# Four attention chunks in one program over a ring of adjacency blocks, in a graph network on one core

## The reference

```python
# layer 0: degree-normalized graph convolution
h = x @ W.T + b;  a = adj + I;  x = layernorm(x + (a * r[:, None] * r[None, :]) @ h)
# layer 1: attention; n = 3327 nodes, h = 8, and d = 128 is the batch of the einsum
q = (x @ Wq.T).reshape(d, n, h)      # k and v alike
a = einsum('dnh,dmh->dnm', q, k) * d ** -0.5 + adj + adj
out = einsum('dnm,dmh->dnh', softmax(a, axis=2), v).reshape(n, h * d) @ Wo.T
x = layernorm(x + out)
# layer 2: graph convolution with bias and relu;  layer 3: attention over edges, by exp and adj.T
```

## Time and profile before

| | us |
|---|---|
| median of three runs | 11376.24 (11374.95 to 11376.49) |
| the profiled execution, its own time | 11372.95 |
| its span | 11371.2 |
| TensorE / VectorE / ScalarE / GpSimd busy | 10347.5 / 9970.1 / 10362.4 / 8141.1 |
| first exponential of the attention to the start of its last one | 844.50 to 10817.38 |

### The profile page before, as it was taken

How to read it: one execution, slowest core, us unless ns; L and a number is a source line. 1 busy time by engine, 2 the same in 40 slices (tenths; PEclk the granted TensorE clock), 3 DMA queues, 4 the chain that set the end, 5 groups by cost and what they waited for, 6 DMA issues and landing times. The chain is left out here.

```text
span 11371.2 us, 371147 instructions
## 1 busy us (share of the span) xinstructions
PE 10347.5 (91%) x138582; PEld 5321.7 (47%) x138582; DVE 9970.1 (88%) x10702; ACT 10362.4 (91%) x8620; POOL 8141.1 (72%) x4114
## 2 busy tenths in 40 slices
PE   5749999999999999999799999999999999999988
PEld 4614555555545555555344444444444444444474
DVE  7348999999989999999799999999899999999958
ACT  3149999999999999999899999999999999999925
POOL 0007888888878888888688888888788888888800
PEclk7979999999999999999899999999999999999999
DMA  8694443433454433433433333333433333333364
GB/s 331 217 254 77 62 62 61 62 61 62 62 94 62 62 61 61 62 61 62 90 54 53 55 55 55 54 54 55 93 54 54 55 55 54 53 55 55 52 197 178
DMA packets 505827, 943.45 MB, mean 83 GB/s; under 512 B 100743, under 2 KB 453390, under 8 KB 454702
## 3 DMA queue, kind: packets, MB, share of 16 engines
q1 hardware_dynamic: 505740, 942.28, 42.4%
HBM read 799.88 MB, written 142.00 MB: 83 GB/s over the span
## 5 line engine op out<-in xcount | busy, mean ns | idle before, releaser
L1101 DVE SCALAR_TENSOR_TENSOR a_probs<-ps,a_adj 128x768 f32<-128x768 f32 (+1 forms) x9216 | 8976.8, 1020 | 776.3 <-PE ps L991 663.4
L1076 POOL TENSOR_TENSOR a_pool_probs<-a_pool_probs,a_adj 128x768 f32<-128x768 f32 (+1 forms) x4096 | 8124.6, 1984 | 1860.7 <-ACT a_pool_probs L1051 1860.7
L1056 ACT ACTIVATE a_probs<-a_probs 128x1536 f32<-128x1536 f32 (+3 forms) x4096 | 8207.4, 2004 | 12.6 <-DVE a_probs L1101 12.2
L991 PE MATMUL ps<-a_q,a_k 34*128 34x384 f32 (+1 forms) x26624 | 4457.4, 406 | 650.6 <-ACT a_pool_probs L1051 367.7
L1051 ACT ACTIVATE a_pool_probs<-ps 128x768 f32<-128x768 f32 (+1 forms) x4096 | 4486.9, 1095 | 32.6 <-PE ps L991 32.5
L1011 PE MATMUL ps<-a_probs,a_v 128*9 128x192 f32 (+1 forms) x73728 | 4012.9, 341 | 0.0
L991 PEld LDWEIGHTS ps<-a_q,a_k 34*128 34x128 f32 x26624 | 2180.5, 185 | 3179.4 <-ACT a_pool_probs L1051 1187.8
L1011 PEld LDWEIGHTS ps<-a_probs,a_v 128*9 128x9 f32 x73728 | 1952.1, 91 | 1273.0 <-issue 126.4
L1011 PE MATMUL ps<-a_pool_probs,a_v 128*9 128x192 f32 (+1 forms) x32768 | 2218.9, 343 | 2.3 <-POOL a_pool_probs L1076 2.2
L1011 PEld LDWEIGHTS ps<-a_pool_probs,a_v 128*9 128x9 f32 x32768 | 489.5, 89 | 986.3 <-issue 980.6
L571 POOL MEMSET v_rows<- 128x512 f32 x2 | 1.9, 1054 | 480.1 <-POOLq L83 480.1
(11 more groups left out here) (177 smaller groups left out, 2104.7 us busy)
## 6 DMA issues: line engine op xcount, KB each, us to landing
a_k<-k_parts SPq DMA_DIRECT2D x2048, 208.0 KB
a_v<-v_ext SPq DMA_DIRECT2D x512, 117.0 KB, 3.4
adj_t<-tr SPq DMA_DIRECT2D x26, 1664.0 KB, 6.4
g0tile<-adj_t SPq DMA_DIRECT2D x26, 1664.0 KB, 6.9
g2tile<-adj_t SPq DMA_DIRECT2D x26, 1664.0 KB, 7.0
nat<-in_adj SPq DMA_DIRECT2D x25, 1663.5 KB, 10.1
e_nat<-in_adj SPq DMA_DIRECT2D x25, 1663.5 KB, 6.8
a_q<-q_parts SPq DMA_DIRECT2D x2048, 12.0 KB
```

The costliest lines, as they stand in the source:

```text
L991: ins = nc.tensor.matmul(ps[:, place + bank:place + bank + half], k_tile[b][row:row + SCORE_ROWS, P * j:P * (j + 1)].bitcast(F32R), q_tile ...
L1056: nc.scalar.activation(sums, sums, ACT.Exp, scale=2.0).then_inc(sums_exped, 1)
L1076: nc.gpsimd.tensor_tensor(flat(k), flat(k), adj_c[:, j, :], ALU.mult).then_inc(multiplied, 1)
L1101: v.scalar_tensor_tensor(out=halves(flat(k)), in0=score(j), scalar=SCALE / 2, in1=halves(adj_c[:, j, :]), op0=ALU.mult, op1=ALU.add).then_ ...
```

## The change

One attention program runs all four chunks, in the same order. The adjacency lies in a ring of 32 blocks (`AdjRing`, `ADJ_SLOTS` = 26 + 6), each of one DMA: with six spare slots part 0 of a chunk (now six blocks) is loaded at the beginning of the chunk before it. Parts 0 and 1 of the first chunk are loaded in the bound phase, and the K tiles are set there too. The factors exp(2 adj) are made once, in the first graph layer, by ScalarE, from the tiles that are loaded there, and kept in the DRAM tensor `factors`; ring blocks of `POOL_BLOCKS` are loaded from it. At a switch K, Q and V of batch 1 are loaded between the parts. K and Q have a semaphore for each half, and stores one for each buffer. In the output phase wo and w2 are loaded behind the first and second row block, and VectorE divides row block 0 before it copies the transposed wo.

```diff
-CHUNK_GROUPS = ((0, 2, 7), (14, 2, 6))
+CHUNKS = ((14, 6), (20, 6), (0, 7), (7, 7))
+GROUPS_OF_CHUNKS = ((6, 2), (7, 2))
+WIDEST = 7
-ADJ_PARTS = ((0, 7), (7, 13), (13, 19), (19, BLOCKS))
+ADJ_PARTS = ((0, 6), (6, 13), (13, 19), (19, BLOCKS))
+ADJ_SLOTS = BLOCKS + 6
@@ gcn_phase, SP and ScalarE
-            with sp.Fori(0, BLOCKS // 2) as t:
-                for b in range(2):
+            for i in range(BLOCKS + 1):
+                b, t = i % 2, i // 2
+                if i < BLOCKS:
                     sp.wait_ge(acc_ready[b], t)
+                    if i >= 2:
+                        sp.wait_ge(made, 2 * (i - 1))
+                    sp.dma_start(tile[b][:, :, :].rearrange("p j q -> p (j q)"), flat_t[i]).then_inc(loaded[b], LOAD)
+                if i:
+                    sp.wait_ge(made, 2 * i)
+                    sp.dma_start(factors[i - 1], factor[1 - b][:, :, :]).then_inc(kept[1 - b], LOAD)
+            per = len(POOL_BLOCKS) // 2
+            for i in range(BLOCKS):
+                b, t = i % 2, i // 2
+                act.wait_ge(loaded[b], (t + 1) * LOAD)
+                if t:
+                    act.wait_ge(kept[b], t * LOAD)
+                for n in range(2):
+                    of = POOL_BLOCKS[per * n]
+                    nc.scalar.activation(factor[b][:, per * n:per * (n + 1), :], tile[b][:, of:of + 3 * per - 2:3, :],
+                                         ACT.Exp, scale=2.0).then_inc(made, 1)
@@ bound_phase, SP and GpSimd
+            for part in ring.EARLY:
+                ring.load(sp, 0, part, True)
+            for b in range(2):
+                nc.gpsimd.memset(k_tile[b][:, :], 1.0)
@@ AdjRing
+    EARLY = (0, 1)
+    def slot(self, c, j):
+        return (BLOCKS * c + j) % ADJ_SLOTS
+    def load(self, sp, c, part, factored):
+        first, nb = CHUNKS[c]
+        for j in range(*ADJ_PARTS[part]):
+            of = self.adj_t[first:first + nb, :, j, :]
+            if factored and j in POOL_BLOCKS:
+                of = self.factors[first:first + nb, :, POOL_BLOCKS.index(j), :]
+            sp.dma_start(self.block(c, j, nb * P).rearrange("p (i q) -> p i q", q=P), of.rearrange("i p q -> p i q")
+                         ).then_inc(self.loaded[part], LOAD)
@@ attention_phase, SP: beginning, and each chunk
-            sp.wait_ge(cleared, 3)
+            load(0, 0, 0)
             load_v(BATCHES - 1, 0)
+            for part in range(len(ADJ_PARTS)):
...
+                if not n_pool or part not in ring.EARLY:
+                    ring.load(sp, 0, part, n_pool > 0)
+            load(0, 1, 1)
             load_v(BATCHES - 2, 1)
+                if more:
+                    sp.wait_ge(ring.loaded[0], ring.ready(c, 0, n_pool > 0))
+                    if c:
+                        used(c - 1, BLOCKS)
+                    ring.load(sp, c + 1, 0, n_pool > 0)
...
                     all_scored(done - 1)
-                    load(0, 0, then)
+                    load(c + 1, 0, 0)
                     sp.wait_ge(batch_summed, done - 1)
                     load_v(BATCHES - 1, 0)
+                    used(c, ADJ_PARTS[1][1] - spare)
+                    ring.load(sp, c + 1, 1, n_pool > 0)
+                sp.wait_ge(stored[1], (done // 2 - 1) * per_store)
+                store(c, done, BATCHES - 2, 0)
                 if more:
+                    used(c, ADJ_PARTS[2][1] - spare)
+                    ring.load(sp, c + 1, 2, n_pool > 0)
                     all_scored(done)
+                    load(c + 1, 1, 1)
+                    used(c, ADJ_PARTS[3][1] - spare)
+                    ring.load(sp, c + 1, 3, n_pool > 0)
                     sp.wait_ge(batch_summed, done)
                     load_v(BATCHES - 2, 1)
@@ attention_phase, TensorE, ScalarE and GpSimd
-                    pe.wait_ge(loaded[b], (pair + of // 2 + 1) * per_load)
+                    for sem in loaded[b]:
+                        pe.wait_ge(sem, (pair + of // 2 + 1) * per_load)
-                        if factors and b == 0:
-                            act.wait_ge(adj_loaded[part_of[j]], (c + 1) * (nb * LOAD))
-                            nc.scalar.activation(adj_c[:, j, :], adj_c[:, j, :], ACT.Exp, scale=2.0
-                                                 ).then_inc(factored, 1)
-            for b in range(2):
-                nc.gpsimd.memset(k_tile[b][:, :], 1.0).then_inc(cleared, 1)
-                                if b == 0:
-                                    pool.wait_ge(factored, c * n_pool + (pool_rank[j] + 1))
+                                if b == 0 and j in (begin for begin, _ in ADJ_PARTS):
+                                    pool.wait_ge(ring.loaded[ring.part_of[j]], ring.ready(c, ring.part_of[j], True))
@@ output_phase, SP, TensorE and VectorE
-            sp.dma_start(w[:, :, :].rearrange("p c h -> p (c h)"), wo).then_inc(w_loaded, LOAD)
             for i in range(BLOCKS):
+                if i == 1:
+                    sp.dma_start(w[:, :, :].rearrange("p c h -> p (c h)"), wo).then_inc(w_loaded, LOAD)
+                if i == 2:
+                    sp.dma_start(second.w[:, :], w2).then_inc(second.w_loaded, LOAD)
...
                 if i == O_BUFS - 1:
-                    sp.dma_start(second.w[:, :], w2).then_inc(second.w_loaded, LOAD)
-            pe.wait_ge(second.w_loaded, LOAD)
+            divide(0)
             dve.wait_ge(w_turned, 1)
             v.tensor_copy(w_t[:, :, :].rearrange("p h f -> p (h f)"), ps[:, 0:QCOLS]).then_inc(w_copied, 1)
-            divide(0)
             divide(1)
```

More of the change, by code:

```diff
@@ L349, in gcn_phase @@
         tmp = [mem.sb(f"{name}tmp{b}", [P, F]) for b in range(2)]
+        factor = [mem.sb(f"{name}factor{b}", [P, len(POOL_BLOCKS), P]) for b in range(2)]
+        made, kept = mem.sem(name + "made"), mem.sems(name + "kept", 2)
         norm = Norm(mem, name)
@@ L790, in _, with __init__, block, ready @@
                                    in1=part[0][:, :].bitcast(F32R), op0=ALU.mult, op1=ALU.subtract).then_inc(rested, 1)
-def attention_phase(nc, keep, group, pool_blocks, adj_t, k_parts, q_parts, q_shift, v_ext, o_rows):
-    first, chunks, nb = group
-    width = nb * P
-    acc_cols = nb * 32
+class AdjRing:
+    EARLY = (0, 1)
+    def __init__(self, mem, adj_t, factors):
+        self.adj_t, self.factors = adj_t, factors
+        self.tile = mem.sb("adj_ring", [P, ADJ_SLOTS, WIDEST * P])
+        self.loaded = mem.sems("adj_ring_loaded", len(ADJ_PARTS))
+        self.part_of = [n for n, (begin, end) in enumerate(ADJ_PARTS) for _ in range(begin, end)]
+    def slot(self, c, j):
+        return (BLOCKS * c + j) % ADJ_SLOTS
+    def block(self, c, j, width):
+        return self.tile[:, self.slot(c, j), 0:width]
+    def load(self, sp, c, part, factored):
[6 more added lines that the diff above has]
+                         ).then_inc(self.loaded[part], LOAD)
+    def ready(self, c, part, factored):
+        times = c + 1 if factored or part not in self.EARLY else c + 2
+        return times * (ADJ_PARTS[part][1] - ADJ_PARTS[part][0]) * LOAD
+def attention_phase(nc, keep, ring, k_tile, pool_blocks, k_parts, q_parts, q_shift, v_ext, o_rows):
     k_of, q_of = by_batch(k_parts), by_batch(q_parts)
@@ L951, in _ @@
                 done = (c + 1) * BATCHES
-                more = c + 1 < chunks
-                then = at + width
                 if more:
                     all_scored(done - 1)
-                    load(0, 0, then)
+                    load(c + 1, 0, 0)
                     sp.wait_ge(batch_summed, done - 1)
                     load_v(BATCHES - 1, 0)
-                    for part, (begin, end) in enumerate(ADJ_PARTS):
-                        sp.wait_ge(added, (done - 1) * n_dve + dve_rank[end - 1] + (not by_pool[end - 1]))
-                        if n_pool:
-                            sp.wait_ge(multiplied, (done - 1) * n_pool + pool_rank[end - 1] + by_pool[end - 1])
-                        load_adj(c + 1, part)
@@ L1089, in _ @@
             v.memset(ps[:, BANK * 6:], 1.0).then_inc(cleared, 1)
-            dve.wait_ge(cleared, 3)
-            with dve.Fori(0, chunks) as c:
-                with dve.Fori(0, turns) as t:
+            dve.wait_ge(cleared, 1)
+            for c, (_, nb) in enumerate(CHUNKS):
+                with dve.Fori(c * turns, (c + 1) * turns) as pair:
                     for k in range(units):
                         b, j = divmod(k, BLOCKS)
-                        batch = (c * turns + t) * 2 + b
-                        if b == 0 and (j == 0 or part_of[j] > part_of[j - 1]):
-                            dve.wait_ge(adj_loaded[part_of[j]], (c + 1) * (nb * LOAD))
+                        batch = pair * 2 + b
+                        if b == 0 and j in (begin for begin, _ in ADJ_PARTS):
+                            part = ring.part_of[j]
+                            dve.wait_ge(ring.loaded[part], ring.ready(c, part, n_pool > 0))
                         if not by_pool[j]:
@@ L1101, in _ @@
```

(4 more changed lines are left out.)

260 lines of the change are left out of this document (131 added, 129 removed).

## The result

The kernel after takes **11739.2 us** (median of 4 runs, 11730.2 to 11741.9), the kernel before, beside it on the same chip, 11376.4: a ratio of 1.0316 with a 95% interval of 1.0303 to 1.0328, 3.2% slower. The forecast was 11302, in a range of 11272 to 11332.

What follows compares the result with a forecast made beforehand. ScalarE was taken to set the period inside chunks, with TensorE close behind. Terms 25 + 5 + 5 + 36 + 5.5 - 1 - 1 = 74.5 us saved from 11372.95 gave 11298, or 11302 with the median's 3.3; range 11272 to 11332.

Steps and rivals of the forecast that it cites:

- The change leaves ScalarE's exponentials in these 4 x 126 batches as they are: Attention: ScalarE's exponentials stay unchanged; only chunk beginnings, what precedes attention and the output phase can move.
- Steady state: Attention batches inside chunks: changed waits and the next chunk's part 0 loads cost 0, all under ScalarE's period.
- The slower rival: Attention batches: TensorE becomes the bound through a second K wait and later order; 11658 at 1 us each; chance 0.04.
- First chunk: Start of attention: earlier memsets and adjacency loads bring batch 1 forward, 25 us saved, 17 to 31.
- Switches: Between attention chunks: 5 us saved at each switch inside a width (0 to 10), 36 between widths (30 to 45).
- First graph layer: Making and storing the factors there: 1 us lost, at most 39 if each store delays a tile load.
- it just fits: First graph layer: stores add 31% to DMA, busy for 0.70 of its time, so 0.92.
- The first layer becomes bound by DMA: Rival, first graph layer: stores delay tile loads by half their time, 20 us, giving 11322; chance 0.07.
- Output and ring's barrier: Output phase: new load order saves 5.5 us (3 to 7); the ring's semaphore clearing and barrier lose 1 (0 to 2).
- Less is won: Rival, switches and first chunk: SP's order keeps part 3 late, first chunk gains only 15, giving 11325; chance 0.13.

Runs made afterwards that it cites:

- the primed kernel: The kernel after, with one exponential of one column ahead of ScalarE's attention loops: 11325.4 us, 0.9955 of the kernel before.
- four tiles: The kernel after with one exponential ahead of ScalarE's loops, plus four tiles for two in the first graph layer, loaded further ahead: 11290.3 us, ratio 0.9924.
- The experiment without early loads: The kernel after with one exponential ahead of ScalarE's loops, but no adjacency blocks loaded in the bound phase: 11347.4 us, ratio 0.9968.

## Why the prediction was wrong

**The step that failed** is the sentence "The change leaves ScalarE's exponentials in these 4 x 126 batches as they are", and with it "*Steady state.* [...] 0". The exponentials are the same, the loop around them is not, and a table load at its head came with that: +414.9 us in 252 batches, which the primed kernel gives back. The two rows of the kernel before that tell of it were there to be read, a count of 13 in a loop of 13 passes and a count of 2 in a loop of two. A load that cost little where it stood (L1048's two take 2.6 us, the first of them ahead of a wait of 14.8 us for DMA) was moved into the innermost loop of the engine that sets the period.

**The slower rival** had the wrong mechanism. It had TensorE become the bound over a second wait for the keys; the primed kernel shows that this wait costs nothing. What held of it is that a small loss in every batch outweighs all the rest: it was 1.64 us a batch, in half of the batches. Its 11658, for a loss of 1 us in all of them, comes near the measured time by chance. It was ScalarE that stopped, and TensorE's clock that turned 1.5 us a turn into 3.3.

**The other terms**, now that the primed kernel shows them by themselves:
- First chunk, 25 saved: 18.5. SP's first load of the keys began 28.7 us behind the root (838.70 - 810.02), where I had 27.6; VectorE began at 838.81, beside it. The Trainium skill's page "Runtime: NRT & Kernel Launch" (Instruction fetch mechanics) says that a taken branch whose target isn't at hand waits for a fetch, and the prediction had worked out from it that SP starts beside VectorE. The trace agrees with that start, and no run shows what the two engines wait for. Part 3 came 2.3 us later than in my working (57.9 behind the root for 55.6); VectorE waits for it at block 20, as 19 is GpSimd's. From there to batch 1's set it was 19.5 for 15.6. The experiment without early loads gives the shorter way to the number: the bytes moved out, 17.8.
- Switches: 4.9 and 35.5 against 5 and 36; 2.5 at the last against 5, within its bounds. Behind the longest wait at the first switch TensorE's granted clock is 0.50 in the primed kernel too (3165 to 3170), so the stretch behind a wait that was shortened stayed slow, as the forecast had kept it. Its reading that the clock is 0.50 in these stretches of the kernel before was too broad: from 3170 to 3175 it reads 1.00.
- First graph layer, 1 lost (0 to 39): 15.0, and 13.1 by itself. Mis-sized by its own reasoning: "it just fits" held for the bytes, but with two tiles a load begins only when a tile is free, and its landing (7.9 us for 6.9) is on the path, 26 times 1 us less what was slack. The rival "The first layer becomes bound by DMA" had 20 for it and the wrong cause, as four tiles show.
- Output and ring's barrier, 4.5 saved: 3.9, of which 2.2 are in the output phase up to its last transposition (116.8 behind the last set for 119.0). The transpositions of `o_rows` begin 6.4 us earlier (some 7 by the forecast) but end only those 2.2 earlier; the forecast had let nearly the whole lead stand.

Without the table loads the change gives 52.6 us (11377.9 to 11325.4) where 74.5 were forecast; 11325 lies in the range that was given. The first layer began between 286.3 and 292.3 in the executions profiled, behind code that is unchanged, which is some of what is left. That 11325 is also the number of the rival "Less is won" is partly chance: of its 23, the first chunk and the switches lost some 10, and 14 are the first layer's.

## What to carry to other kernels

Read the rows that no source line asks for, table loads above all, with their counts: a count that equals a loop's passes says where the compiler puts them, and a change of the loop structure or of what runs ahead of a loop can move one into the hottest body. One dummy activation of the loop's function ahead of it settles it. When an engine at 96% waits on another at 100%, price a stop of the second not by its length alone but also by what the first one's clock does behind it.

## What the runs showed of the hardware

- A stop of ScalarE of 0.32 us in each turn costs 0.32; of 0.80 it costs 1.2 on average; of 1.5 it costs 2.9 to 3.3. The excess comes in steps of about 1.45 us, one or two a turn, and only in turns in which TensorE's granted clock falls to 0.50.
- The Trainium skill's page "ScalarE: Activation LUTs" (What ACT_TABLE_LOAD costs) gives 1283 ns for a load, and with the drain 2.66 us for a switch to a different set. The 1283 is here to the digit. A load between exponentials cost 1.5 us where TensorE's clock held, and at a switch from copies to the square root in the kernel before 1.31 us pass from the end of the one (254.41) to the start of the other (255.72); so here the measured figures are the ones to use.
- TensorE's granted clock fell after some waits of 1.64 us and not after others of the same length (938 and 975), behind the waits of 1.0 us in 35 of 126 turns, and in none of the 126 turns of the kernel whose waits were 0.5 at most. What decides between equal waits these runs don't show, and it wasn't tried.
